# Vision-transformer layer with experts: softmax reciprocals in another PSUM bank, load order at the handover, and weighted groups on GpSimd

## The chip, the cores and the metric

The kernel runs on one core of a Trainium2 chip. The metric is the device time of one execution in microseconds (us), median of several runs. The core has TensorE (matmuls), VectorE, ScalarE, GpSimd and SyncE, each with its own in-order instruction queue; they meet only through semaphores. SBUF is the on-chip memory, PSUM the banks into which TensorE writes, and 16 DMA engines move data to and from device memory.

## The reference

Sixteen images x[16, 4, 128, 256] in float32 go through three parts.

```
tok:  w = x.sum(groups).mean(256); h = gelu(w @ w1.T + b1); w = softmax over 4 groups of (h @ w2.T + b2)
      h[b] = sum over g of x[b, g] * w[g, b]                         # 128 tokens x 256
attn: n = layernorm(h); 16 heads of 16; softmax(q k^T / 4 + relative bias) v;  h += ctx @ Wo.T
moe:  n = layernorm(h); gates = softmax(n @ Wg + bg), the best 2 of 8 experts, normalised
      h += sum over the 2 experts of gate * (gelu(n @ W1[e] + b1[e]) @ W2[e] + b2[e])
```

## The kernel before

The 128 tokens of an image lie on the 128 partitions. The work has three stages.

**Setup** loads the first images and turns the weights.

**Image steps.** step(i) for i = 0 to 16 is a software pipeline over three images, written out by hand on each engine: the front of image i (project_qk, project_v, key masks, scores, biased scores, exponentials of chunks 0 and 1), the back of image i-1 (exponentials of chunks 2 and 3, transposes called context, values, reciprocals, normalise), and the late part of image i-2 (out_project, residual, second norm, gate logits). The four groups of an image are weighted and added one or two images ahead: ScalarE writes the first weighted group (first_group(i + 2), line 553) and VectorE adds groups 1 to 3 in select_groups(i + 1) (line 1107), followed by the statistics of the first norm. GpSimd computes the two rstd (line 434), half of the masked keys (mask_keys, line 267), and in steps 7 to 15 sends out the token records of batches already ranked, by indirect DMA (scatter_records, line 445). The table record_steps says which: two DMAs a step, but four in steps 12 and 14. Ahead of each even-numbered one GpSimd waits until all earlier ones have landed (`scat`).

The softmax reciprocals are widened by VectorE (srcw), turned by TensorE (spread_sums, line 778) into the lower half of the bank psQK, and copied by ScalarE (r_evac, line 567) to rT; VectorE's normalise multiplies psCX by rT. turn_x (line 769) turns the next image's normed tokens into the upper half of psQK, and so waits for r_sb. Then follow values(b, 1), scores(i, 1) and gate_logits in TensorE's queue.

After step 2 TensorE computes the selection logits of images 4 to 15 (select_logits, line 741), once keep_logits(0) has freed the bank (lg_sb); VectorE's select_weights and ScalarE's select_exps make the weights tsel from them, and ScalarE's first_group(4) stands ahead of its step 3.

**Expert tiles.** 39 tiles of 128 token records each: SyncE loads a tile's records (`sel<-meta_dram`) and the expert's first weights (load_w1, 1 MB); GpSimd gathers the tokens (line 482) and scatters the results (line 491); TensorE turns them (turn_xs, line 935) and multiplies (hidden, line 947, and second, line 959). The first 14 tiles need only the records of images 0 to 10. SyncE's queue at the handover is, in order: load_w1(0, 0), load_w1(1, 1), store_xn2(13), one store, the wait for the records' DMAs, records 0 and 1, the wait for s_min and the load of b2 (1 MB), records 2, store_xn2(14), records 3, load_w1(2, 0).

Of the kernel before, what the change touches and what calls it, by code (L numbers as in the profile page):

```python
# [63 lines left out]
def vit_layer_kernel(nc, x, tok_w1, tok_b1, tok_w2, tok_b2, Wq, Wk, Wv, Wo, rel_emb,  # L64
# [8 lines left out]
    with ExitStack() as ctx:  # L73
# [6 lines left out]
        def sem(name):  # L80
            return ctx.enter_context(nc.semaphore(name))
# [119 lines left out]
        waited = {e: sem(f"waited_{n}") for e, n in ((nc.vector.engine, "dve"), (nc.gpsimd.engine, "pool"),  # L201
                                                    (nc.scalar.engine, "act"))}
        dv_const = sem("dv_const")
        setup_ps = sem("setup_ps")
        wT_sb, tokw_sb, b1T_sb = sem("wT_sb"), sem("tokw_sb"), sem("b1T_sb")
        rel_ps = sem("rel_ps")
# [88 lines left out]
        def _(sp):  # L295
# [43 lines left out]
            with sp.Fori(0, E - 2) as e:  # L339
# [5 lines left out]
            load_w2(E - 1)  # L345
            sp.wait_ge(tables_ok, 1)
            load_w1(0, 0)
            load_w1(1, 1)
            store_xn2(B - 3)
            sp.dma_start(sum_dram.ap()[N_TOK:N_TOK + P, :], hcol(0)).then_inc(h_out, 16)  # L350
            sp.wait_ge(scat, 16 * TOPK * EARLY_B)
            load_records(0)
            next_records(1)
            sp.wait_ge(s_min, NCH * B)
            sp.dma_start(relb[:, 0:E * D], b2.rearrange("e d -> (e d)").partition_broadcast(P)) \
                .then_inc(b2_in, 16)
            next_records(2)
            store_xn2(B - 2)
            next_records(3)
            load_w1(2, 0)  # L360
            store_xn2(B - 1)
            next_records(4)
# [26 lines left out]
        def _(pool):  # L389
# [41 lines left out]
            def rstd_of(i, ln, n, done):  # L431
                pool.wait_ge(ln, n)
                pool.wait_ge(dv_const, 1)
                pool.tensor_tensor(rstd[i][:, :], ve[i][:, :], minus_half[:, :], ALU.pow) \  # L434
                    .then_inc(done, 1)

            def scatter_records(g, a, b):
# [4 lines left out]
                for i in range(BATCHES[g][0] * TOPK + a, BATCHES[g][0] * TOPK + b):  # L442
                    if i >= 2 and i % 2 == 0:
# [6 lines left out]
            record_steps = ((7, 0, 0, 2), (8, 0, 2, 4), (9, 0, 4, 6), (10, 0, 6, 8), (11, 1, 0, 2), (12, 1, 2, 6),  # L450
                            (13, 1, 6, 8), (14, 2, 0, 4), (15, 2, 4, 6))

            def step(i, nxt=True, late=True):

                if nxt:
                    rstd_of(0, ln1, LN1_N * (i + 1) + 3, ln1_pow)
                mask_keys(pool, i, 1)
                if late:
                    rstd_of(1, ln2, LN2_N * (i - 2) + 3, ln2_pow)
                for at, g, a, b in record_steps:  # L460
                    if at == i:
                        scatter_records(g, a, b)
# [53 lines left out]
        def _(act):  # L516
# [46 lines left out]
            def r_evac(b):  # L563
                act.wait_ge(r_ps, b + 1)
                if later(b):
                    act.wait_ge(ctx_ok, b)
                act.copy(rT[:, :], psQK[:, 0:DC * S]).then_inc(r_sb, 1)

            def qk_evac(b):
                act.wait_ge(qk_ps, b + 1)  # L570
# [133 lines left out]
        def _(pe):  # L704
# [55 lines left out]

            def turn_x(b):

                if later(b, 1):
                    pe.wait_ge(r_sb, b - 1)
                pe.wait_ge(ln1, LN1_N * (b + 1))
                if later(b):
                    pe.wait_ge(qk_sb, b)
                for c in range(DC):
                    i = pe.transpose(psQK[:, (DC + c) * S:(DC + c + 1) * S], xn1[:, c * P:(c + 1) * P],
                                     ident[:, :])  # L770
                i.then_inc(x1T_ps, 1)

            def spread_sums(b):

                pe.wait_ge(s_wide, b + 1)
                pe.wait_ge(qk_sb, min(b + 2, B) if isinstance(b, int) else b + 2)
                for c in range(DC):
                    i = pe.transpose(psQK[:, c * S:(c + 1) * S],
                                     srcw[:, c * P:(c + 1) * P], ident[:, :])
                i.then_inc(r_ps, 1)  # L780

# [43 lines left out]
            def values(b, w):  # L825
                if w == 0:
                    pe.wait_ge(v_sb, b + 1)
                    if later(b):
                        pe.wait_ge(ctx_ok, b)
                pe.wait_ge(pT_sb, NCH * b + 2 * w + 2)  # L830
                for j in range(2):
                    for n in range(CH):
                        k = 2 * n + j
                        i = pe.matmul(psCX[n * PART:(n + 1) * PART, w * S:(w + 1) * S],  # L834
                                      v_s[:, v_at(w * HPC + k):v_at(w * HPC + k) + PART],
                                      pT[k // CH][:, k % CH * S:(k % CH + 1) * S], start=(j == 0), stop=(j == 1))
                i.then_inc(pv_ps, 2)
# [41 lines left out]
                pe.matmul(psG[:, RKC:RKC + n * E], before[:, :], counts[:, E:(n + 1) * E],  # L879
                          start=False, stop=True).then_inc(rank_ps, 1)  # L880

            def step(i, u, front=True, back=True, late=True, nxt=True, batch=None, sums=False):

                if front:
                    project_qk(i)
# [24 lines left out]
                    values(i - 1, 1)  # L910
                if front:
                    scores(i, 1)
                if late:
                    gate_logits(i - 2)

# [3 lines left out]
            pe.wait_ge(b1T_sb, 1)  # L919
            step(1, 1, late=False, sums=True)  # L920
            image_sums(3, 2)
            step(2, 0)
            pe.wait_ge(lg_sb, 1)
            select_logits(1, NG, B)
            placed = {first + n + 3: g for g, (first, n) in enumerate(BATCHES[:-1])}
            for i in range(3, B - 1):
                step(i, i % 2, batch=placed.get(i))
# [45 lines left out]
                    turn_xs(j + 1, 1 - u, k + u)  # L973
                second(j - 1, 1 - u, e)

            pe.wait_ge(r_sb, B)
            turn_xs(0, 0, 0)
            hidden(0, 0, 0)
            turn_xs(1, 1, 0)
# [23 lines left out]
        def _(dve):  # L1003
# [92 lines left out]

            def select_groups(b, done=None):

                dve.wait_ge(tok_first, b + 1)
                for g in range(1, G):  # L1100
                    if g == 2 and done is not None:
                        top_two(*done)
                    if g == 3 and done is not None:
                        top_index(*done)
                    if g > 1:
                        dve.wait_ge(tok_acc, (G - 1) * b + g - 1)
                    dve.scalar_tensor_tensor(out=hcol(b), in0=xw2[:, bass.ds(b * (G * D) + g * D, D)],
# [311 lines left out]
```

## Time and profile before

| | |
|---|---|
| median of 3 runs | 538.91 us (538.74 to 540.49) |
| profiled execution, own time | 538.68 us |
| its span | 536.9 us |
| TensorE matmul busy | 484.0 us, 90% |
| VectorE busy | 219.0 us, 41% |
| ScalarE busy | 262.6 us, 49% |
| GpSimd busy | 178.9 us, 33% |
| mean granted clock of TensorE | 0.969 |

Times in rows are microseconds from the span's start. PE is TensorE (PEld its weight loads, which overlap its matmuls), DVE VectorE, ACT ScalarE, POOL GpSimd, SPq the DMA queue of SyncE. In a timeline a row is: start, duration, engine, line, operation, out<-in, shape, count, and in brackets the engine's idle time just before it with what ended it. The chain of waits is the work that ended last, followed back from the end.

### The profile page before, as it was taken

Reading aid. Unit: us, or ns where it says so; the run is one execution under the profiler, and the core shown is the slowest. Engines: PE = TensorE matmul, PEld = TensorE weight load, DVE = VectorE, ACT = ScalarE, POOL = GpSimd, SP = SyncE. Lnnn points to the kernel's source line nnn. Section 1 sums busy time; section 2 is a strip of 40 time slices with the busy share of each in tenths; the row PEclk is TensorE's granted clock in tenths of the full one; section 3 lists DMA queues with packets and bytes.
Section 4 is the critical chain, followed back from the end, with each engine's and each line's share of the span. In section 5 each row is a group of like instructions: output and inputs, shape, how many; then the busy total and the mean of one; then the engine's idle time right before and its main releaser. Section 6 shows DMA issues by size and latency. Waiting matters only on the chain.

```text
span 536.9 us, 13085 instructions
## 1 busy us (share of the span) xinstructions
PE 484.0 (90%) x3742; PEld 409.8 (76%) x3743; DVE 219.0 (41%) x1068; ACT 262.6 (49%) x1003; POOL 178.9 (33%) x186
## 2 busy tenths in 40 slices
PE   4779899999999999499999999999999999999980
PEld 2557676666766665289998989999999999999960
DVE  2665788887887887422241111111111111111110
ACT  1347689889998888632432223332233332323310
POOL 3020113233334633213265533333333333333321
PEclk9979899999999999879999999999999999999995
DMA  8890030313313046536656665666766666666515
GB/s 273 244 351 31 21 99 22 102 38 102 85 36 100 22 120 204 172 112 193 183 140 171 194 169 148 187 187 192 195 180 175 165 178 184 195 189 174 138 20 166
DMA packets 51004, 78.61 MB, mean 146 GB/s; under 512 B 10528, under 2 KB 39472, under 8 KB 50768
## 3 DMA queue, kind: packets, MB, share of 16 engines
q1 hardware_dynamic: 40160, 66.80, 38.4%
q0 software_dynamic: 8592, 10.58, 11.8%
q10 hardware_dynamic: 2208, 0.71, 0.6%
q8 instruction: 20, 0.33, 0.3%
q14 instruction: 24, 0.20, 0.2%
HBM read 68.27 MB, written 11.90 MB: 149 GB/s over the span
## 4 chain that ended last, share of the span: by engine, by line
PE 73%; issue 9%; DMA 5%; DVE 4%; POOL 3%; ACT 3%; POOLq 0%; DVEq 0%; SPq 0%; ACTq 0%
PE psVO L959 23%; PE psS L947 12%; PE psP L947 12%; PE psP L822 5%; PE psQK L789 5%; PE psS L812 4%; DMA fold<-xn_dram,sel 3%; PE psCX L834 2%; PE psVO L845 2%; PE psVO L800 2%; PE psQK L935 2%; ACT prob L592 2%; DVE prob L1127 2%; POOL meta_dram L445 2%; PE psG L725 1%
## 5 line engine op out<-in xcount | busy, mean ns | idle before, releaser
L959 PE MATMUL psVO<-xw,prob 128*128 x624 | 141.8, 380 | 0.8 <-DVE fold L1349 0.8
L959 PEld LDWEIGHTS psVO<-xw,prob 128*128 128x128 f32 x624 | 115.5, 190 | 15.8 <-issue 1.2
L491 POOL DMA_INDIRECT sum_dram<-fold,sel x39 | 62.0, 1591 | 163.4 <-DMA sel<-meta_dram 103.6
L592 ACT ACTIVATE prob<-prob,smin 128x128 f32<-128x128 f32 x256 | 100.4, 405 | 6.1 <-DVE smin L1127 5.8
L679 ACT ACTIVATE prob<-psS,b1T 128x128 f32<-128x128 f32 x160 | 45.8, 369 | 99.5 <-PE psS L947 99.5
L679 ACT ACTIVATE prob<-psP,b1T 128x128 f32<-128x128 f32 x152 | 43.5, 369 | 92.6 <-PE psP L947 87.9
L947 PEld LDWEIGHTS psS<-fold,w1c 128*128 128x128 f32 x640 | 76.6, 197 | 1.9 <-DVE fold L1344 1.0
L947 PE MATMUL psS<-fold,w1c 128*128 128x128 f32 x640 | 77.1, 280 | 0.6 <-DVE fold L1344 0.6
L947 PEld LDWEIGHTS psP<-fold,w1c 128*128 128x128 f32 x608 | 70.8, 192 | 0.9
L947 PE MATMUL psP<-fold,w1c 128*128 128x128 f32 x608 | 71.0, 275 | 0.0
L434 POOL TENSOR_TENSOR rstd<-ve,minus_half 128x1 f32<-128x1 f32 x32 | 23.9, 747 | 136.5 <-DVE ve L1090 133.1
L1349 DVE TENSOR_TENSOR fold<-psVO,relb 128x256 f32<-128x256 f32 x39 | 16.6, 425 | 122.1 <-PE psVO L959 118.9
L1344 DVE COPY fold<-psQK 128x256 f32<-128x256 f32 x39 | 16.6, 425 | 112.5 <-PE psQK L935 112.5
L1127 DVE CUSTOM_DVE_ANT_0 prob<-psS,relb 128x128 f32<-128x128 f32 x256 | 56.7, 286 | 13.2 <-PE psS L812 12.5
L592 ACT ACTIVATION_READ_ACCUMULATOR prob<-prob,smin 128x1 f32 x256 | 52.0, 203 | 0.0
L581 ACT COPY pT<-psP 128x512 f32<-128x512 f32 x64 | 36.1, 594 | 20.9 <-PE psP L822 20.9
L482 POOL DMA_INDIRECT fold<-xn_dram,sel x39 | 39.0, 1001 | 19.4 <-issue 10.9
L812 PE MATMUL psS<-kbd,qkT 64*128 64x512 f32 x128 | 37.1, 655 | 4.7 <-DVE smin L1127 2.3
L445 POOL DMA_INDIRECT meta_dram<-meta,pos x32 | 32.4, 1011 | 24.6 <-DMA meta_dram<-meta,pos 12.2
L822 PEld LDWEIGHTS psP<-ident,prob 128*128 128x128 f32 x256 | 28.1, 141 | 15.7 <-issue 8.3
L822 PE MATMUL psP<-ident,prob 128*128 128x128 f32 x256 | 37.9, 280 | 0.7 <-ACT prob L592 0.7
L789 PE MATMUL psQK<-x1T,wT 128*128 128x128 f32 x256 | 34.2, 289 | 0.5 <-ACT x1T L561 0.5
(166 smaller groups left out, 491.7 us busy)
## 6 DMA issues: line engine op xcount, KB each, us to landing
w1c<-in_L_ffn_W SPq DMA_DIRECT2D x39, 1024.0 KB
xw<-in_x SPq DMA_DIRECT2D x16, 512.0 KB, 8.1
xw<-in_L_ffn_W SPq DMA_DIRECT2D x8, 1024.0 KB, 5.9
sum_dram<-h_all SPq DMA_DIRECT2D x17, 128.0 KB
xn_dram<-xn SPq DMA_DIRECT2D x16, 128.0 KB
out<-sum_dram SPq DMA_DIRECT2D x4, 512.0 KB, 5.9
relb<-in_L_ffn_b SPq DMA_DIRECT2D x1, 1024.0 KB, 5.5
sel<-meta_dram SPq DMA_DIRECT2D x39, 2.0 KB
```

What stands on the lines that cost most here:

```text
L445: pool.indirect_dma_start(out=meta_dram.ap()[:, :], out_offset=bass.IndirectOffsetOnAxis(ap=pos[:, i:i + 1], axis=0), in_=meta[:, i * META ...
L482: pool.indirect_dma_start(out=xs[j % 2], out_offset=None, in_=xn_dram.ap()[0:EARLY_B * S if j < EARLY else N_TOK, :], in_offset=bass.Indir ...
L491: pool.indirect_dma_start(out=sum_dram.ap()[0:EARLY_B * S if j < EARLY else N_TOK + P, :], out_offset=bass.IndirectOffsetOnAxis(ap=row_no[ ...
L581: act.copy(pT[c % 2][:, :], psP[c % 2][:, :]).then_inc(pT_sb, 1)
L592: i = act.activation(blk, blk, ACT.Exp, bias=smin[:, k:k + 1], scale=-1.0, accum_out=ssum[:, k:k + 1])
L679: i = act.activation(hT[u][:, c * P:(c + 1) * P], hidden_ps[u][c // 4][:, c % 4 * P:(c % 4 + 1) * P], ACT.Gelu, bias=b1T[:, bass.ds(e * HC ...
L789: i = pe.matmul(psQK[:, (t * DC + oc) * S:(t * DC + oc + 1) * S], wT[t][:, ic * D + oc * P:ic * D + oc * P + P], x1T[:, ic * S:(ic + 1) * ...
L812: pe.matmul(psS[r][:, :], qkT[rows, w * S:(w + 1) * S], kbd[rows, w * CH * S:(w + 1) * CH * S], start=True, stop=True).then_inc(s_ps, 1)
L822: i = pe.transpose(psP[c % 2][:, n * S:(n + 1) * S], pr[:, h * S:(h + 1) * S], ident[:, :])
L947: i = pe.matmul(hidden_ps[u][c // 4][:, c % 4 * P:(c % 4 + 1) * P], w1c[u][:, d * H + c * P:d * H + (c + 1) * P], xsT[:, d * P:(d + 1) * P ...
L959: i = pe.matmul(psVO[:, 0:D], hT[u][:, c * P:(c + 1) * P], xw2[:, bass.ds(e * (HC * D) + c * D, D)], start=(c == 0), stop=(c == HC - 1))
L1127: i = dve.tensor_tensor_reduce(prob[u % 2][:, h * S:(h + 1) * S], psS[c % 2][:, n * S:(n + 1) * S], relb[:, h * S:(h + 1) * S], 1.0, HIGHE ...
```

## The change

Three edits, and a fourth that moves a small piece.

1. spread_sums writes the upper half of the bank psCX instead of the lower half of psQK. r_evac reads there. turn_x no longer waits for r_sb; values(b, 1) does. The waits of spread_sums for qk_sb and of the first tile for r_sb go.
2. SyncE: load_w1(1, 1) and store_xn2(14) move behind records 1 and 2, and the load of b2 behind records 3.
3. For images 5 to 15 GpSimd weights groups 1 to 3 in place with one product over 768 columns and adds them to the first group with three sums, in step b - 2, behind its rstd and ahead of that step's records. VectorE's select_groups(b) keeps only the wait, the statistics and the two operations on the gate logits of a finished image.
4. select_logits for images 4 to 15 moves into step 2, ahead of gate_logits(0), waiting for x2T_sb instead of lg_sb.

```diff
@@ SyncE @@
             load_w1(0, 0)
-            load_w1(1, 1)
             store_xn2(B - 3)
...
             next_records(1)
+            next_records(2)
+            load_w1(1, 1)
+            store_xn2(B - 2)
+            next_records(3)
             sp.wait_ge(s_min, NCH * B)
             sp.dma_start(relb[:, 0:E * D], b2.rearrange("e d -> (e d)").partition_broadcast(P)) \
                 .then_inc(b2_in, 16)
-            next_records(2)
-            store_xn2(B - 2)
-            next_records(3)
@@ GpSimd @@
+            def select_groups(b):
+
+                pool.wait_ge(tok_first, b + 1)
+                pool.wait_ge(tok_acc, (G - 1) * b)
+                x_of = xw2[:, b * (G * D) + D:(b + 1) * (G * D)]
+                x_of = [x_of] + [x_of[:, g * D:(g + 1) * D] for g in range(G - 1)]
+                pool.tensor_tensor(chunks(x_of[0], G - 1, D), chunks(x_of[0], G - 1, D),
+                                   over(tsel[:, B:G * B].rearrange("p (g b) -> p g b", g=G - 1)[:, :, b], D),
+                                   ALU.mult).then_inc(tok_part, 1)
+                pool.wait_ge(tok_part, 2 * (b - NG) - 1)
+                pool.tensor_tensor(x_of[1], x_of[1], x_of[2], ALU.add).then_inc(tok_part, 1)
+                pool.tensor_tensor(hcol(b), hcol(b), x_of[3], ALU.add).then_inc(tok_acc, 1)
+                pool.wait_ge(tok_part, 2 * (b - NG))
+                pool.wait_ge(tok_acc, (G - 1) * b + 1)
+                pool.tensor_tensor(hcol(b), hcol(b), x_of[1], ALU.add).then_inc(tok_acc, 2)
+
             def step(i, nxt=True, late=True):
...
                 if late:
                     rstd_of(1, ln2, LN2_N * (i - 2) + 3, ln2_pow)
+                if NG < i + 2 < B:
+                    select_groups(i + 2)
                 for at, g, a, b in record_steps:
@@ ScalarE @@
-                act.copy(rT[:, :], psQK[:, 0:DC * S]).then_inc(r_sb, 1)
+                act.copy(rT[:, :], psCX[:, DC * S:2 * DC * S]).then_inc(r_sb, 1)
@@ TensorE @@
             def turn_x(b):
 
-                if later(b, 1):
-                    pe.wait_ge(r_sb, b - 1)
...
             def spread_sums(b):
...
-                pe.wait_ge(qk_sb, min(b + 2, B) if isinstance(b, int) else b + 2)
                 for c in range(DC):
-                    i = pe.transpose(psQK[:, c * S:(c + 1) * S],
+                    i = pe.transpose(psCX[:, (DC + c) * S:(DC + c + 1) * S],
@@ values @@
+                else:
+                    pe.wait_ge(r_sb, b + 1)
                 pe.wait_ge(pT_sb, NCH * b + 2 * w + 2)
@@ TensorE's step @@
+                if select:
+                    pe.wait_ge(x2T_sb, i - 1)
+                    select_logits(1, NG, B)
                 if late:
                     gate_logits(i - 2)
...
-            step(2, 0)
-            pe.wait_ge(lg_sb, 1)
-            select_logits(1, NG, B)
+            step(2, 0, select=True)
...
-            pe.wait_ge(r_sb, B)
             turn_xs(0, 0, 0)
@@ VectorE @@
             def select_groups(b, done=None):
 
+                if done is not None:
+                    top_two(*done)
+                if b > NG:
+                    dve.wait_ge(tok_acc, (G - 1) * (b + 1))
+                    norm_stats(0, hcol(b), ln1, LN1_N * b)
+                    if done is not None:
+                        top_index(*done)
+                    return
+                if done is not None:
+                    top_index(*done)
                 dve.wait_ge(tok_first, b + 1)
                 for g in range(1, G):
-                    if g == 2 and done is not None:
-                        top_two(*done)
-                    if g == 3 and done is not None:
-                        top_index(*done)
```

## Rows read from the trace of the kernel before

**Rows 1.** Chain of waits, 133 to 146 us: start, duration, what.
```profile
133.84 1.89 PE psQK L789 x16
...
141.78 0.26 ACT rT L567
...
144.10 0.26 ACT x2T L609
```

**Rows 2.** Timeline of a regular step, 137 to 149 us, all engines.
```profile
137.65 0.69 DVE L267 TENSOR_TENSOR kbd<-qkT,pmask 128x512 f32<-128x512 f32 x1
137.80 0.97 POOL L434 TENSOR_TENSOR rstd<-ve,minus_half 128x1 f32<-128x1 f32 x1 [5.85 <-DVE ve L1090]
...
138.44 0.42 DVE L1156 TENSOR_TENSOR h_all<-h_all,psVO 128x256 f32<-128x256 f32 x1
...
138.75 1.03 POOL L267 TENSOR_TENSOR kbd<-qkT,pmask 128x512 f32<-128x512 f32 x1
...
142.04 0.52 ACT L553 ACTIVATE h_all<-xw,tsel 128x256 f32<-128x256 f32 x1
...
142.21 0.44 PE L769 MATMUL psQK<-ident,xn 128*128 128x128 f32 x2 [0.51 <-ACT rT L567]
...
148.98 1.09 POOL L434 TENSOR_TENSOR rstd<-ve,minus_half 128x1 f32<-128x1 f32 x1 [5.86 <-DVE ve L1090]
```

**Rows 3.** Instructions of lines 1107 and 267: count, ns min/median/max, first and last start.
```profile
L1107 DVE SCALAR_TENSOR_TENSOR h_all<-xw,tsel,h_all x48: 464/478/486, 18.9 to 193.7; 128x256 f32<-128x256 f32 x48
...
L267 POOL TENSOR_TENSOR kbd<-qkT,pmask x16: 1030/1034/1547, 28.7 to 209.1; 128x512 f32<-128x512 f32 x16
```

**Rows 4.** Timeline of GpSimd, ScalarE and VectorE in steps 12 and 13.
```profile
176.90 0.52 ACT L553 ACTIVATE h_all<-xw,tsel 128x256 f32<-128x256 f32 x1
...
177.16 0.98 POOL L445 DMA_INDIRECT meta_dram<-meta,pos  x1 [0.30 <-issue]
...
181.16 0.96 POOL L445 DMA_INDIRECT meta_dram<-meta,pos  x1 [3.01 <-DMA meta_dram<-meta,pos]
...
186.06 0.55 POOL L434 TENSOR_TENSOR rstd<-ve,minus_half 128x1 f32<-128x1 f32 x1
...
187.57 0.29 DVE L1127 CUSTOM_DVE_ANT_0 prob<-psS,relb 128x128 f32<-128x128 f32 x1
...
188.65 0.40 ACT L592 ACTIVATE prob<-prob,smin 128x128 f32<-128x128 f32 x1
```

**Rows 5.** Timeline from step 2 to step 3, 62 to 70 us.
```profile
62.80 0.97 PEld L741 LDWEIGHTS psG<-sel 128*128 128x128 f32 x8 [1.69 <-DVE lg_all L1168]
...
63.68 3.42 PEld L789 LDWEIGHTS psQK<-x1T,wT 128*128 128x128 f32 x16
...
63.90 0.21 DVE L1068 TENSOR_TENSOR sel<-psG,tb 128x48 f32<-128x48 f32 x1 [1.15 <-PE psG L741]
...
68.12 1.06 ACT L581 COPY pT<-psP 128x512 f32<-128x512 f32 x2
...
69.90 0.38 PEld L834 LDWEIGHTS psCX<-pT,v_s 128*32 128x32 f32 x16 [0.33 <-issue]
```

**Rows 6.** Stretch 64 to 66 us: busy per engine, clock, DMA share, GB/s.
```profile
64.00:66.00 2.00, 2.00 (x11) 2.00 (x11) 1.21 (x6) 0.55 (x2) 0.00 (x0) 0.50 0.00 0
```

**Rows 7.** Chain of waits at the handover, 200 to 260 us.
```profile
215.52 3.57 DMA meta_dram<-meta,pos
...
222.37 5.95 DMA fold<-xn_dram,sel
...
229.84 6.03 PE psS L947 x32
```

**Rows 8.** Timeline of SyncE's DMA queue at the handover.
```profile
208.43 1.70 SPq L330 DMA_DIRECT2D w1c<-in_L_ffn_W  x2
...
222.45 0.43 SPq L355 DMA_DIRECT2D relb<-in_L_ffn_b  x1
```

**Rows 9.** Timeline of TensorE at the first tile.
```profile
228.57 0.66 PE L935 MATMUL psQK<-ident,fold 128*128 128x128 f32 x2 [5.90 <-DMA fold<-xn_dram,sel]
```

More of the change, by code:

```diff
@@ L203, in vit_layer_kernel @@
         dv_const = sem("dv_const")
+        tok_part = sem("tok_part")
         setup_ps = sem("setup_ps")
@@ L880, in ranks, with step @@
                           start=False, stop=True).then_inc(rank_ps, 1)
-            def step(i, u, front=True, back=True, late=True, nxt=True, batch=None, sums=False):
+            def step(i, u, front=True, back=True, late=True, nxt=True, batch=None, sums=False, select=False):
                 if front:
```

## The prediction

> **What bounds the kernel now.** I read the busy table first: TensorE works nine tenths of the span, GpSimd a third, VectorE two fifths. Then the chain of waits, which splits the span in two stages. The sixteen image steps end near 222 us, the 39 expert tiles fill the rest, and in the tiles TensorE hardly stops. The change touches no tile instruction, so the question is what happens to the image steps and to the handover.
>
> A regular image step takes 11.18 us (GpSimd's rstd at 137.80 and 148.98 [rows 2]). Its chain goes in a ring: project_qk, transposes and projections, values, scores, then ScalarE's copies of the transposed probabilities and of the reciprocals, its first weighted group, four exponentials, the copy of x2T, and the gate logits ahead of the next project_qk [rows 1]. ScalarE hands over to TensorE at 144.10 + 0.26 = 144.36. Neither VectorE's three weighted adds nor the wait of turn_x on the reciprocals' copy, 0.51 us long [rows 2], has a place in that ring.
>
> **Reciprocals in the context's bank.** turn_x no longer waits for r_sb, but values(b, 1) now does, since it writes the bank that ScalarE's copy reads. So TensorE still waits for the same event (the copy that starts at 141.78 [rows 1]), with turn_x's 0.44 us [rows 2] moved ahead of it. values(1) and scores(1) come up to 0.4 us earlier, but gate_logits, next in TensorE's queue, waits for x2T, which ScalarE copies only after the four exponentials. The gain is swallowed there. I cost it at 0; bounds 0 and -0.4 us a step (12 such steps, -4.8).
>
> **Weighted groups on GpSimd.** VectorE loses three operations of 478 ns per image [rows 3], 11 images: 15.8 us of VectorE time, all ahead of the kbd product, which waits for ScalarE's copy of q and k anyway. Worth 0 in regular steps, perhaps 0.1 in each of the three gate steps (VectorE ends last there), -0.3 together.
>
> GpSimd gains per image one product over 768 columns and three sums over 256. The nearest row is its own kbd product, 512 columns in 1034 ns [rows 3], 2.02 ns a column: 1.55 us for the product, 0.52 us for each sum. Three waits on its own results lie between; rows 4 show 0.30 us between two of its DMA instructions, so I take about 0.25 each: 1.55 + 1.56 + 0.75 = 3.9 us. The bounds are 3.1 (no gaps) and 4.6 (0.55 us a sum, 0.45 a gap).
>
> It starts only when ScalarE's first group of image i+2 is there, 142.04 + 0.52 = 142.56 [rows 2], and ends about 146.5. VectorE's statistics follow; before, they released GpSimd's rstd at 148.98, 2.5 us later, and GpSimd had idled 5.86 us for it [rows 2], so nothing is lost. In steps 7 to 11 and 13 two record DMAs stand behind the select in its queue: 0.2 + 1.0 + 0.30 + 0.98 = 2.5 us (the last two from rows 4, the first two taken as like), to 149.0. That is a tie with 148.98: no cost, but no slack either.
>
> The Trainium skill (GPSIMD Engine Reference, 3.1 Elementwise) speaks against such a move: it gives a two-input add on GpSimd as 1.96 times VectorE's time and keeps elementwise work on VectorE. The trace has 1.03 against 0.69 us for the same product (138.75 and 137.65 [rows 2]), a ratio of 1.5. By the page's ratio the select would be, as an estimate, 6.4 us, and all steps with records would be late by some 2 us; the trace's own ratio decides here.
>
> **Step 12: where it hurts.** This step issues four record DMAs, and the third waits until the first two have landed. Before, the second went out at 177.16, the third after 3.01 us of waiting at 181.16 [rows 4]. Now the select stands in front, and itself waits for the first group that ends at 176.90 + 0.52 = 177.42 [rows 4]. Working: select to 181.3; two DMAs 2.5, to 183.8; landing 3.0, to 186.8; two DMAs 0.96 + 0.30 + 1.0, to 189.1; 0.35 to the rstd of image 14 (0.55, to 190.0); the second half of kbd 1.03, to 191.1; the rstd of image 11, to 191.7. That last one ended at 186.06 + 0.55 = 186.6 before [rows 4]: 5.1 us later. VectorE's queue holds first_norm, second_norm, the masks and then biased(0) behind it, which began at 187.57, and ScalarE's exponentials behind that at 188.65, straight after its own work [rows 4]. So there is no slack: step 13 starts its ring 5.0 us late. Bounds 4.2 (select 3.1) and 5.8.
>
> TensorE idles those 4 to 5 us (turn_xn2 waits for second_norm). After an idle of 1.69 us [rows 5] its granted clock was 0.50, the 1.2 GHz level, in 64 to 66 us [rows 6], and project_qk's weight loads took 3.42 us [rows 5] against 1.89 for the matmuls of a step at full clock [rows 1]. I add 1.5 us for this; bounds 0 and 2.5. Together +6.5.
>
> Steps 14 and 15 get no select, and select(15) in step 13 starts behind the late rstd (191.7) and ends with its two DMAs near 198, while step 14 wants its rstd more than 3 us after that by now, so the delay doesn't grow.
>
> **select_logits(1) earlier.** Before, TensorE waited 1.69 us for lg_sb, then ran select_logits (62.80), then project_qk (63.68) at half clock; values(0) of that step began at 69.90 [rows 5]. Now select_logits runs right behind scores(1), at 62.80 less the idle and the gate logits' half microsecond, near 60.6. VectorE had idled 1.15 us for it when it began the weights at 63.90 [rows 5]; that idle goes, and ScalarE, which waits for the weights, starts 1.1 us earlier. TensorE was the later of the two at values(0); with project_qk at 62.1 it no longer is: ScalarE's second copy ended at 69.18 [rows 5], now at 68.1, and values(0) follows it, -1.75. I take -1.6; bounds -1.1 and -1.8.
>
> **Handover to the tiles.** The records' chain was: DMA of the last early record pair 215.52 + 3.57, records 0, gather 0 issued 222.37 and landed 5.95 us later, hidden(0) 6.03 us [rows 7]; TensorE began at 228.57 after 5.90 us idle [rows 9]. The 1 MB load of b2 was issued at 222.45 [rows 8], beside the gather. Now records 1 and 2 stand in front of w1(1,1) and b2, so the first megabyte is issued near 224.1. No row shows a gather without load beside it; the nearest from below is the record pair, 3.57 us from the start of its second issue, from above the 5.95 itself. I take 3.6, nearer the pair, because the first 1.7 us after the issue are free of load: -2.4. The record pair before it flew beside both w1 loads (208.43 [rows 8]); now only one is there, worth 0 to 1 us, I take 0.4. Sum -2.8, bounds -1.0 and -4.0. TensorE then still idles 3.1 us, so hidden(0) keeps its 6.03 us. w1(1,1) is needed only behind hidden(0), 7 us later: hidden.
>
> **Sum.** 0 - 0.3 + 6.5 - 1.6 - 2.8 = +1.8 us on the profiled execution's 538.68: 540.5. The median of the runs stands 0.23 higher, so 540.7.
>
> **Rivals.**
> (a) *The handover pays more than the stall costs* (faster). Place: from 207 to 234 us. If the gather and the last records save 4.0 us or more, TensorE idles below 1.9 us, close to the 1.69 us of rows 5, and hidden(0) may run in 3.6 instead of 6.03: -6.4 instead of -2.8. It decides from about 4 us saved. For it: the load of b2 leaves the gather's way, and the gather is most of the idle. Against: w1(0,0) still flies beside the records. With the stall at 6.5: -1.9, 537.0; without the clock's loss in step 13: 535.5.
> (b) *GpSimd's port.* VectorE's kbd product (two SBUF inputs, 137.65) and GpSimd's rstd (137.80) overlapped, and the rstd took 0.97 us [rows 2] instead of 0.55 [rows 4]; but the residual add out of PSUM (138.44, 0.42) overlapped with GpSimd's kbd (138.75, 1.03), which took no longer than its median [rows 2, 3]. The select runs beside biased, which reads PSUM and SBUF. If these excluded each other, each regular step would lose about 1 us: +11, 551. The Trainium skill (SBUF — State Buffer, SBUF: two separate sides) calls the shared pair an exclusive lock, but only against VectorE operations with two SBUF inputs or in a two-port mode; by that rule biased is free, and the rows agree as far as they go.
> (c) *The released wait pays after all:* 0.38 us in 12 steps, -4.6, and with the rest 536.1. Against it stands the chain, where turn_x is absent.
> (d) *The stall isn't there,* because the records of step 12 find GpSimd free: only if the select took well under 1 us. Then 538.9 - 4.7 = 534.2.
>
> **How the numbers follow.** Forecast 0.57 (its own range 538.5 to 543.5), (a) 0.18, (b) 0.10, (c) 0.08, (d) 0.03, small mixtures the rest. Range 535.8 to 545.0: it takes in (a), (c) and the bounds of the stall and the clock, and leaves (b) and (d) out. Measurement tells about 0.3% (1.6 us) from no change. Faster by more: (a) mostly, (c), (d): 0.23. Within: the lower half of the forecast: 0.31. Slower: 0.46.
>
> **What would show it.** In the changed kernel: GpSimd's select lasting near 3.9 us and starting when ScalarE's first group ends; a GpSimd queue in step 12 whose fourth record DMA ends near 188 and an rstd behind it, with ScalarE idle for 4 to 5 us ahead of step 13's exponentials on VectorE's smin; regular steps of 11.2 us still; project_qk of step 3 1.5 us earlier; gather 0 in under 4 us. It is wrong if step 13 starts without idle, if the regular steps change by more than 0.2 us, or if TensorE idles as long as before at the handover.

## The result and the profile after

The changed kernel takes 542.5 us (median of 8 runs, 540.76 to 543.14) against 539.46 us before (8 runs, 538.74 to 540.74): a ratio of 1.0043 with a 95% interval of 1.0027 to 1.006, that is 1.5 to 3.2 us slower. The prediction was 540.7 us, range 535.8 to 545.0, with "slower" the likeliest of the three signs. Its sum was made against the profiled execution: 538.68 and +1.8. The profiled execution of the changed kernel took 540.76 us, so +2.1 there. This execution was also the fastest of its eight; the rows below account for the +2.1, and what the other runs have on top is shown by no profile.

The step times come from the weight loads of project_qk, which open every step on TensorE. The table gives the length of each stretch in us.

| stretch (from project_qk to project_qk) | before | after | difference | forecast |
|---|---|---|---|---|
| step 1 | 13.18 | 12.85 | -0.3 | 0 |
| step 2, to 63.68 and to 61.59 | 13.51 | 11.70 | -1.8 | -1.6 |
| step 3 | 12.69 | 12.54 | -0.15 | 0 |
| gate steps 6 and 10 together | 22.81 | 23.23 | +0.4 | -0.2 |
| regular steps | 11.18 | 11.17 | 0 | 0 |
| step 13, to the project_qk of step 14 | 11.35 | 17.97 | +6.6 | +6.5 for both |
| step 14 | 11.89 | 13.47 | +1.6 | |
| handover, project_qk of step 15 to the first tile's transposes | 25.59 | 21.75 | -3.8 | -2.8 |
| tiles, to the end of the span | 308.4 | 307.8 | -0.6 | 0 |

The differences add up to +1.9 us, as much as the spans (536.9 and 538.8) differ. The two large terms are those of the forecast, each larger than forecast, in opposite directions. (In a gate step the expert gates of a batch of finished images are computed as well; the handover is the passage from the last image step to the first expert tile.)

The GpSimd queue through steps 12 and 13, where [rows 4] had shown two record DMAs, a wait of 3.01 us and two more:

```profile
175.65 1.47 POOL L460 TENSOR_TENSOR xw<-xw,tsel 128x768 f32<-128x768 f32 x1 [2.05 <-ACT h_all L572]
...
178.78 0.73 POOL L468 TENSOR_TENSOR h_all<-h_all,xw 128x256 f32<-128x256 f32 x1 [0.17 <-POOL h_all L465]
179.68 1.04 POOL L446 DMA_INDIRECT meta_dram<-meta,pos  x1 [0.17 <-issue]
181.02 0.98 POOL L446 DMA_INDIRECT meta_dram<-meta,pos  x1 [0.30 <-issue]
183.42 0.96 POOL L446 DMA_INDIRECT meta_dram<-meta,pos  x1 [1.41 <-DMA meta_dram<-meta,pos]
...
185.66 0.57 POOL L435 TENSOR_TENSOR rstd<-ve,minus_half 128x1 f32<-128x1 f32 x1
186.21 1.03 POOL L268 TENSOR_TENSOR kbd<-qkT,pmask 128x512 f32<-128x512 f32 x1
187.21 0.55 POOL L435 TENSOR_TENSOR rstd<-ve,minus_half 128x1 f32<-128x1 f32 x1
187.73 1.46 POOL L460 TENSOR_TENSOR xw<-xw,tsel 128x768 f32<-128x768 f32 x1
189.27 0.72 POOL L464 TENSOR_TENSOR xw<-xw 128x256 f32<-128x256 f32 x1
189.95 0.78 POOL L465 TENSOR_TENSOR h_all<-h_all,xw 128x256 f32<-128x256 f32 x1
190.90 0.72 POOL L468 TENSOR_TENSOR h_all<-h_all,xw 128x256 f32<-128x256 f32 x1 [0.17 <-POOL h_all L465]
```

The select of image 14 lasts from 175.65 to 179.51, 3.86 us, and every record DMA of the step comes after it. The third one waits only 1.41 us, less than half of before. The rstd of image 11 (187.21) ends at 187.76, and the select of image 15 starts at once behind it. What this does to VectorE is in VectorE's timeline of the same stretch:

```profile
186.35 3.80 DVE L1112 TENSOR_SCALAR xn<-h_all,mv,rstd 128x256 f32<-128x256 f32 x2 [1.71 <-POOL rstd L435]
190.07 0.73 DVE L1220 TENSOR_TENSOR hot<-e_no,picked 128x48 f32<-128x48 f32 x1
...
191.09 0.29 DVE L1151 CUSTOM_DVE_ANT_0 prob<-psS,relb 128x128 f32<-128x128 f32 x1
```

The two normalisations (`xn`, the first norm of image 14 and the second norm of image 11) take 3.80 us together. In the regular step at 138.37 the same pair takes 0.75 us. The group of line 1112 over the whole execution says how unusual that is (count, ns min/median/max); the 3.00 us are the first of the two, from 186.35 to 189.35, and the second lasts 0.88 us from 189.27:

```profile
L1112 DVE TENSOR_SCALAR xn<-h_all,mv,rstd x32: 405/409/3000, 23.0 to 241.8; 128x256 f32<-128x256 f32 x32
```

ScalarE waits for the biased scores; its timeline:

```profile
192.16 0.40 ACT L611 ACTIVATE prob<-prob,smin 128x128 f32<-128x128 f32 x1 [5.42 <-DVE smin L1151]
```

and TensorE for the second normalisation; its weight loads:

```profile
190.20 0.29 PEld L878 LDWEIGHTS psG<-ident,xn 128*128 128x128 f32 x2 [4.78 <-DVE xn L1112]
...
195.82 3.53 PEld L805 LDWEIGHTS psQK<-x1T,wT 128*128 128x128 f32 x16
```

The stretches of 2 us show TensorE idle from 186 to 190 and its granted clock behind that (window, length, busy of PE, PEld, DVE, ACT, POOL, clock, DMA share, GB/s):

```profile
186.00:188.00 2.00, 0.00 (x0) 0.00 (x0) 1.65 (x1) 0.74 (x3) 2.00 (x4) 1.00 0.02 1
188.00:190.00 2.00, 0.00 (x0) 0.00 (x0) 2.00 (x2) 0.00 (x0) 1.92 (x3) 0.83 0.00 0
190.00:192.00 2.00, 1.80 (x20) 1.31 (x20) 1.89 (x12) 0.00 (x0) 1.66 (x3) 0.50 0.34 114
...
196.00:198.00 2.00, 2.00 (x11) 2.00 (x11) 1.82 (x15) 1.78 (x9) 0.00 (x0) 0.50 0.14 29
198.00:200.00 2.00, 2.00 (x13) 2.00 (x13) 0.35 (x4) 0.31 (x1) 0.56 (x1) 0.61 0.00 0
200.00:202.00 2.00, 2.00 (x13) 1.82 (x12) 0.69 (x1) 2.00 (x8) 1.55 (x1) 1.00 0.04 8
```

The clock is at the 1.2 GHz level from 190 to past 198, so the end of step 13 and the opening of step 14 run at half clock: project_qk's loads take 3.53 us instead of 1.87.

The handover, in the chain of waits of the changed kernel, answers to [rows 7]; the third row is of TensorE's timeline and answers to [rows 9]:

```profile
222.53 2.12 DMA meta_dram<-meta,pos
...
227.85 2.97 DMA fold<-xn_dram,sel
...
232.35 6.08 PE psS L966 x32
```

```profile
231.07 0.66 PE L954 MATMUL psQK<-ident,fold 128*128 128x128 f32 x2 [2.09 <-DMA fold<-xn_dram,sel]
```

The gather lands in 2.97 us instead of 5.95 and the last record pair in 2.12 instead of 3.57. TensorE idles 2.1 us instead of 5.9, and hidden(0) still takes 6.1 us.

Last, the step 2 to step 3 passage, in TensorE's weight loads, against [rows 5]:

```profile
60.26 0.97 PEld L760 LDWEIGHTS psG<-sel 128*128 128x128 f32 x8 [0.81 <-ACT x2T L628]
...
61.59 1.87 PEld L805 LDWEIGHTS psQK<-x1T,wT 128*128 128x128 f32 x16
```

### The profile page after: what moved, and what is told of

Read it like the earlier page. It is cut to its first block, busy times and chain, and to the rows that moved or that the text cites. A ratio compares the mean times of both kernels' runs of the same rounds, so it can differ in the third digit from the quotient of the medians.

```text
span 538.8 us, 13118 instructions
## 1 busy us (share of the span) xinstructions
PE 485.4 (90%) x3742; PEld 411.6 (76%) x3743; DVE 212.9 (40%) x1035; ACT 262.4 (49%) x1003; POOL 216.4 (40%) x230
## 3 DMA queue, kind: packets, MB, share of 16 engines
q0 software_dynamic: 8592, 10.58, 11.7%
## 4 chain that ended last, share of the span: by engine, by line
PE 68%; issue 10%; DVE 7%; POOL 4%; ACT 4%; DMA 4%; POOLq 0%; DVEq 0%; SPq 0%; ACTq 0%
PE psVO L978 23%; PE psS L966 12%; PE psP L966 12%; PE psQK L805 4%; PE psP L838 4%; PE psS L828 3%; DVE prob L1151 2%; DMA fold<-xn_dram,sel 2%; ACT prob L611 2%; POOL meta_dram L446 2%; PE psVO L816 2%; PE psVO L863 2%; PE psQK L954 2%; PE psG L884 1%; DVE xn L1112 1%
## 5 line engine op out<-in xcount | busy, mean ns | idle before, releaser
L611 ACT ACTIVATE prob<-prob,smin 128x128 f32<-128x128 f32 x256 | 100.0, 401 | 11.7 <-DVE smin L1151 11.7
L435 POOL TENSOR_TENSOR rstd<-ve,minus_half 128x1 f32<-128x1 f32 x32 | 19.5, 608 | 82.0 <-DVE ve L1108 80.2
L611 ACT ACTIVATION_READ_ACCUMULATOR prob<-prob,smin 128x1 f32 x256 | 50.8, 198 | 0.0
```

The costliest lines, as they stand in the source:

```text
L611: i = act.activation(blk, blk, ACT.Exp, bias=smin[:, k:k + 1], scale=-1.0, accum_out=ssum[:, k:k + 1])
```

## The experiments

The theory behind the runs: the change is three gains or nothings (loads, select_logits, bank) and one loss, the select that stands ahead of step 12's four record DMAs. The rival was that GpSimd's work costs everywhere, through the port that it shares with VectorE. The kernel before was timed again beside the experiments: 538.98 us (7 runs) beside the first four, 539.44 us (26 runs) beside the others; each ratio is against the one beside it.

**The select of image 14 between the record pairs.** GpSimd sends the first pair, then adds the groups while the pair is in flight, then sends the second pair.

```diff
+                if i == 12:
+                    scatter_records(1, 2, 4)
+                    select_groups(14)
+                    scatter_records(1, 4, 6)
+                    return
                 if NG < i + 2 < B:
                     select_groups(i + 2)
```

> The changed kernel with one edit: in step 12 GpSimd sends the first pair of records ahead of image 14's weighted groups and the second pair behind them, instead of all four behind. If the queue of step 12 is the cause of the late step 13 (my theory), the pair falls into GpSimd's 2.1 us of waiting for the first group, its landing is hidden under the select, and the next rstd comes about 182.7 instead of 185.7 us: step 13 takes 11.3 to 12.0 us instead of 18.0, step 14 no longer runs project_qk at half clock, and the time is 534 to 535.5 us against 542.5 of the changed kernel. If the stall came from the weighted groups running beside VectorE's norms (the shared port), the order of the records does little: 540 to 542.5.

Measured 530.85 us (4 runs, 530.03 to 532.94) against 538.98: ratio 0.9845 (0.9815 to 0.9875). All GpSimd selects are still there, in every regular step; only the order in one step differs from the changed kernel. GpSimd's timeline:

```profile
173.94 1.04 POOL L446 DMA_INDIRECT meta_dram<-meta,pos  x1 [0.23 <-issue]
175.28 0.98 POOL L446 DMA_INDIRECT meta_dram<-meta,pos  x1 [0.30 <-issue]
176.27 1.49 POOL L460 TENSOR_TENSOR xw<-xw,tsel 128x768 f32<-128x768 f32 x1
...
180.31 0.99 POOL L446 DMA_INDIRECT meta_dram<-meta,pos  x1 [0.15 <-issue]
...
184.33 0.55 POOL L435 TENSOR_TENSOR rstd<-ve,minus_half 128x1 f32<-128x1 f32 x1 [0.16 <-DVE ve L1113]
```

The wait for the landing is gone (the select fills it), the rstd of image 11 now waits for VectorE and not VectorE for it, and project_qk goes 177.97, 189.30, 200.99: step 13 takes 11.33 us and step 14 takes 11.69. The stall is the loss: the rival, for which selects cost in every step, is out. (Inside the stalled step GpSimd does hold VectorE up; the experiment on the select of image 15 below gives its share.) The run is 3 to 5 us better than expected: the expectation had counted on 7 to 8.5 us against the changed kernel, and the medians are 11.7 apart. The profiled executions are 7.8 us apart (540.76 and 532.94); steps 13 and 14 alone give 8.4 of it (23.02 us for 31.44), and the rest goes the other way. The first profile is of the fastest run of its kernel and the second of the slowest of its own, so where the rest of the medians' difference lies is shown by neither.

**The groups back on VectorE**, the rest of the change kept.

```diff
-                if NG < i + 2 < B:
-                    select_groups(i + 2)
```

(and VectorE's select_groups as before.)

> The changed kernel with the weighted groups 1 to 3 back on VectorE; the other three edits stay. My theory: image steps as before the change but 2.2 us earlier from step 3 on, no stall in step 13, handover 3.8 us shorter, so 539.5 - 6.0 = 533.5 us. If the handover's saving in the changed kernel was only the other side of the stall (records and loads had more time to land), it goes too: about 537.

Measured 531.5 us (530.45 to 534.42), ratio 0.9869 (0.9822 to 0.9915). That is 2 us better than expected. The intervals of this run and the first overlap for the most part. So moving the adds to GpSimd gains nothing that can be measured even where it does no harm: the "0" of the forecast for regular steps holds from this side too. It also says that the three other edits are worth about 7.5 us together, and that the handover's saving doesn't need the stall.

**The groups on GpSimd alone**, on the kernel before.

```diff
+                if NG < i + 2 < B:
+                    select_groups(i + 2)
                 for at, g, a, b in record_steps:
```

> The kernel before with only the weighted groups on GpSimd. My theory: the whole cost stands here, 8.2 us in steps 13 and 14 and 0.4 in the gate steps, and nothing is given back: 548 us. If part of the stall is absorbed at the handover (where DMAs and not the image steps end last), 543 to 545.

Measured 548.32 us (545.57 to 550.86), ratio 1.019 (1.0148 to 1.0232). Step 13 takes 17.95 us (180.56 to 198.51), the same as in the changed kernel, and step 14 takes 13.32. The profiled execution was the fastest of the four (545.57), so of the median's +9.3 us its rows account for 6.9. The row of project_qk at the start of step 14:

```profile
198.51 3.30 PEld L808 LDWEIGHTS psQK<-x1T,wT 128*128 128x128 f32 x16
```

The loss belongs to this edit alone and needs none of the others.

**The load order alone**, on the kernel before.

```diff
-            load_w1(1, 1)
             store_xn2(B - 3)
...
             next_records(1)
+            next_records(2)
+            load_w1(1, 1)
```

(with b2 behind records 3, as in the change.)

> The kernel before with only the new order of SyncE's loads and records. My theory: gather 0 lands in 3 us instead of 6, and the last record pairs a little earlier: 539.5 - 3.8 = 535.7 us, with TensorE idle 2 us instead of 6 ahead of the first tile. If the saving needs the stall, 538 or more; if TensorE's clock then holds at 2.4 GHz through the first tile, 533.5.

Measured 534.54 us (534.1 to 535.66), ratio 0.9916 (0.9887 to 0.9944): -4.4 us, where I had the handover at -2.8. Its chain of waits:

```profile
217.11 2.12 DMA meta_dram<-meta,pos
219.96 1.62 DMA sel<-meta_dram
222.47 2.80 DMA fold<-xn_dram,sel
...
226.81 5.88 PE psS L947 x32
```

The gather lands in 2.80 us here and in 2.85 to 2.97 in the other four kernels with the new order whose chains show it, against 5.80 to 6.04 in the four with the old order. The record pair lands in 2.10 to 2.12 us in all five with the new order. With the old one it took 2.98, 3.25, 3.57 and, in the kernel with the groups on GpSimd alone, 6.21 us. So both gains belong to the load order, the gather's is the steadier, and the pair's depends on which execution with the old order it is set against.

**select_logits alone**, on the kernel before.

```diff
-            step(2, 0)
-            pe.wait_ge(lg_sb, 1)
-            select_logits(1, NG, B)
+            step(2, 0, select=True)
```

> The kernel before with only select_logits for images 4 to 15 moved ahead of gate_logits(0). My theory: TensorE's 1.7 us of idle and the half clock behind it go, step 2 takes 11.7 instead of 13.5 us from project_qk to project_qk: -1.9 us, 537.2. If later waits take it back, 538.5 to 539.5.

Measured 536.09 us (7 runs, 535.0 to 539.12), ratio 0.9936 (0.9916 to 0.9957), -3.4 us. The profile shows project_qk of step 3 at 62.78 and a start of step 2 at 51.03, 11.75 us apart, against 13.51 before: -1.8 us, the forecast's mechanism. The other 1.6 us of the median have no row: this profiled execution was the slowest of the seven, and longer in the tiles.

**The bank alone**, on the kernel before.

```diff
-                act.copy(rT[:, :], psQK[:, 0:DC * S]).then_inc(r_sb, 1)
+                act.copy(rT[:, :], psCX[:, DC * S:2 * DC * S]).then_inc(r_sb, 1)
```

(and the waits of TensorE as in the change.)

> The kernel before with only the reciprocals in the context's bank, and the wait for r_sb moved from turn_x to values(b, 1). My theory: the step's ring does not pass through turn_x, so nothing: 539.2 within 0.7 us. If the released wait pays 0.38 us in 12 steps, 534.6.

Measured 538.45 us (12 runs, 537.4 to 540.1), ratio 0.9982 (0.996 to 1.0005): -1.0 us, with no change at all inside the interval. TensorE's weight loads in the regular step at 140 us show why there is no more:

```profile
140.99 0.25 PEld L767 LDWEIGHTS psQK<-ident,xn 128*128 128x128 f32 x2
141.77 0.38 PEld L833 LDWEIGHTS psCX<-pT,v_s 128*32 128x32 f32 x16 [0.53 <-ACT rT L567]
142.49 0.33 PEld L809 LDWEIGHTS psS<-kbd,qkT 64*128 64x128 f32 x4 [0.35 <-issue]
143.96 0.52 PEld L865 LDWEIGHTS psG<-wg_s,x2T 128*128 128x128 f32 x4 [1.14 <-ACT x2T L609]
```

turn_x runs ahead of the wait, the wait for the reciprocals' copy stands in front of values instead, and what values and scores gain is lost again at gate_logits, which waits 1.14 us for ScalarE's x2T. Rival (c) is out. What is there lies in single steps: 12.85 instead of 13.18 us for step 1, 11.68 instead of 11.89 for step 14.

**The first record pair ahead of the select in every step**, on the changed kernel.

```diff
+                for g, a, b in mine:
+                    scatter_records(g, a, min(b, a + 2))
                 if NG < i + 2 < B:
                     select_groups(i + 2)
+                for g, a, b in mine:
+                    if b > a + 2:
+                        scatter_records(g, a + 2, b)
```

> The changed kernel with the first pair of each step's records ahead of the weighted groups, in every step and not in step 12 alone. My theory: the pair falls into GpSimd's 2.1 us of waiting for the first group; only step 12 was short, so the time is that of the version with step 12 alone, 530.9, within 1 us. If the tie of steps 7 to 11 (records end just when the rstd is due) costs something each time, 529 to 530.

Measured 532.44 us (530.84 to 534.27), ratio 0.987 (0.9835 to 0.9904). The median is 1.5 us above the expected 530.9, half a microsecond outside the margin given, but its interval and the first run's overlap. So in the steps with two record DMAs no effect of the order can be told from none, as the forecast's "tie" had it.

**The select of image 15 held back until the masks of step 13 are done**, on the changed kernel. This is the test of the 3.80 us pair: the stall by the queue stays, and VectorE's delay by the select goes.

```diff
+                if i == 13:
+                    pool.wait_ge(gate_step, GATE_N * 2 + MASKS_AT)
                 if NG < i + 2 < B:
                     select_groups(i + 2)
```

> The changed kernel with one wait more: in step 13 GpSimd starts the weighted groups of image 15 only when VectorE has finished second_norm and the masks of that step. The records of step 12 stay where they are. In the changed kernel's trace VectorE's two normed outputs of that step last 3.80 us instead of 0.75, and end only when GpSimd's product over 768 columns and its first sum are through. If GpSimd's weighted groups hold VectorE up there (shared port), biased(0) of step 13 starts 2.4 us earlier and the step takes 15.6 us instead of 18.0; time 540.1 instead of 542.5. If VectorE waited for something else (GpSimd's rstd alone), nothing changes or the added wait costs: 542.5 to 544.

Measured 538.51 us (10 runs, 537.98 to 541.2), ratio 0.9993 (0.9972 to 1.0014), 4.0 us below the changed kernel by the medians (542.5 and 538.51, measured at different times) where 2.4 were expected. The profiled executions are 2.3 us apart, and only 1.1 of that lies in steps 13 and 14. VectorE's timeline:

```profile
185.96 1.05 DVE L1114 TENSOR_SCALAR xn<-h_all,mv,rstd 128x256 f32<-128x256 f32 x1 [1.70 <-POOL rstd L435]
187.55 0.41 DVE L1114 TENSOR_SCALAR xn<-h_all,mv,rstd 128x256 f32<-128x256 f32 x1 [0.55 <-POOL rstd L435]
187.88 0.20 DVE L1222 TENSOR_TENSOR hot<-e_no,picked 128x48 f32<-128x48 f32 x1
```

With GpSimd quiet, the second normalisation takes 0.41 us again and `hot` 0.20. From the end of the rstd (187.41) to the first biased operation (188.37) it is 0.96 us; in the changed kernel, from 187.76 to 191.09, it is 3.33. So the GpSimd select held VectorE up by 2.4 us. Step 13 took 15.65 us (expected 15.6). Half of this is given back in step 14, which took 14.65 us instead of 13.47: TensorE resumes earlier but runs at half clock just as far. Windows of this run:

```profile
190.00:192.00 2.00, 1.70 (x4) 0.54 (x4) 1.62 (x6) 2.00 (x11) 1.83 (x3) 0.50 0.68 146
...
196.00:198.00 2.00, 2.00 (x11) 2.00 (x11) 0.40 (x1) 0.76 (x2) 0.53 (x2) 0.50 0.04 8
198.00:200.00 2.00, 2.00 (x10) 1.75 (x9) 0.29 (x1) 1.73 (x7) 1.19 (x1) 0.68 0.00 0
```

The clock comes back between 198 and 200 us here as in the changed kernel, although TensorE is back at work at 188.0 and not at 190.2. So more of step 14 lies before that point: the transposes and part of the out_project as well as project_qk.

**The clock at the handover.** The first experiment's profile bears on rival (a), which put the return of the clock in hidden(0) below 1.9 us of idle time. Its row of TensorE's timeline and its windows:

```profile
222.89 0.41 PE L959 MATMUL psQK<-ident,fold 128*128 128x128 f32 x2 [1.66 <-DMA fold<-xn_dram,sel]
223.92 5.47 PE L971 MATMUL psS<-fold,w1c 128*128 128x128 f32 x32 [0.61 <-DVE fold L1373]
```

```profile
222.00:224.00 2.00, 0.49 (x3) 0.28 (x3) 0.68 (x4) 0.00 (x0) 0.34 (x1) 1.00 0.59 81
224.00:226.00 2.00, 2.00 (x12) 2.00 (x13) 0.21 (x2) 0.00 (x0) 0.96 (x1) 0.66 0.93 342
226.00:228.00 2.00, 2.00 (x12) 2.00 (x11) 0.00 (x0) 0.77 (x4) 0.00 (x0) 0.50 1.11 408
228.00:230.00 2.00, 2.00 (x17) 1.95 (x17) 0.36 (x1) 0.85 (x4) 0.00 (x0) 0.99 0.98 405
```

Idle pauses of 1.66 and 0.61 us, with TensorE busy 0.49 of 2 us at 222 to 224, and the clock still falls, if later. hidden(0) took 5.47 us here, 6.08 in the changed kernel, against 3.57 for the same work at full clock in later tiles. In the kernel with the groups back on VectorE TensorE was idle for only 0.18 us ahead of the first tile's transposes and 1.19 us behind them, and the clock fell there too:

```profile
222.00:224.00 2.00, 0.72 (x3) 0.51 (x4) 1.77 (x10) 0.48 (x2) 0.70 (x1) 0.76 0.59 141
```

Its hidden(0) took 6.78 us. No run here kept the clock through the handover.

## Why the prediction came out as it did

**The regular steps, the bank, rival (b) and (c).** Right. Regular steps stay at 11.17 us; the select takes 3.86 us (forecast 3.9) from the end of ScalarE's first group. That agreement is partly luck: the product took 1.47 us (forecast 1.55), the three sums 2.19 (1.56), and the gaps 0.2 (0.75). The 6.4 us that the prediction sets beside its 3.9 comes without its working; scaled as its own sum is, with 1.96 for 1.5 and the same gaps, it is 4.8. Where the step has a record pair, the first rstd stands right behind it (146.01 + 0.98, then 147.01) and the step is no longer than before: the tie was one. Rival (b) asked whether VectorE's biased operations and GpSimd's select exclude each other. They don't: at 191.09 biased runs beside the select at its usual 0.29 us.

**Steps 13 and 14: the mechanism right, all three of its terms wrong in size.** Counted from the project_qk of step 13:

| term | forecast | measured |
|---|---|---|
| rstd of image 11 later | +5.1 | +3.0 (ends 9.91 us in, was 6.9) |
| VectorE between that rstd and biased | 0 (-0.1) | +2.4 |
| half clock | +1.5 | +2.8 (1.26 in step 13, 1.58 in step 14) |
| sum | +6.5 | +8.2 |

The first two errors almost cancel: the first biased operation came 5.4 us later, against the 5.1 that the forecast had for the rstd and with it for the start of step 13. That this number came out was luck.

The first term was too high. Measured from project_qk (179.70 before, 177.85 after), the select was forecast to end 1.6 us in and the first pair 4.1 us in; they ended 1.66 and 4.15 us in. Then the forecast carried the landing of the pair over unchanged, 3.0 us, where it took 1.41: 1.6 of the 2.1 us by which the term is too high, the rest being small gaps that weren't there. Why it landed sooner stays open. Before the change the stores of step 12 went out just ahead of the pair's second DMA (176.32 and 176.86 against 177.16), and in the changed kernel they are over by then. But with the stores at the same distance the wait was 3.48 and 3.47 us with the loads and with select_logits alone, and only 1.84 with the bank alone and 1.77 with the groups back on VectorE. So the stores alone don't set it, and the 3.0 carried over was one value of several.

The second term is the step that failed. The forecast said of select(15) that it "starts behind the late rstd (191.7) and ends with its two DMAs near 198, while step 14 wants its rstd more than 3 us after that", and so cost it at nothing. It asked only who waits for the select and not whom the select holds up while it runs. In a regular step the select falls beside VectorE's biased operations and ctxT, which read PSUM and kept their times (0.29 and 0.43 us at 142.28 and 140.91). The stall shifted it against VectorE's queue, so that it fell on the two normalisations and the masks, whose tensor operands are in SBUF. The experiment that held it back showed the 2.4 us. The Trainium skill (SBUF — State Buffer, "SBUF: two separate sides") has this as a rule: VectorE and GpSimd share a port pair, which one instruction locks for its whole length. The trace agrees in that the operation was held: 3.00 us for one of 0.41. The Trainium skill names there operations with two SBUF inputs and those in a two-port mode, and further down ("Who interferes with whom") tensor_scalar among the candidates; the forecast weighed the rule on biased alone, where it is free. One instruction's length isn't enough for the 3.00 us, though. The operation started 0.14 us into GpSimd's kbd product (186.21) and ended 0.16 us behind the product that GpSimd had begun at 187.73, so three GpSimd instructions in a row went ahead of it. In the run that held the select back it started 0.15 us into the same kbd product and took 1.05 us. What lets several go first isn't shown by any run here.

Not every operation on SBUF is held. The statistics of the norm, one SBUF input of the same 128x256, take 427 to 429 ns all 32 times in the kernel before, also where GpSimd's kbd product (184.91 to 185.94) runs beside them:

```profile
185.04 0.43 DVE L1085 BATCH_NORM_STATS2 st<-h_all 128x6 f32<-128x256 f32 x1
```

The third term lay above the upper bound of 2.5. The forecast had taken it from one project_qk at half clock (3.42 for 1.89 us). The half clock lasted over 8 us here and also held the transposes, values and scores of step 13 and the project_qk of step 14. From ScalarE's first exponential to the next project_qk it was 3.66 us instead of 2.40 (188.65 to 191.05 before), the 1.26; step 14 has the 1.58, nearly all of it project_qk's 3.53 for 1.87.

**select_logits.** Forecast -1.6, measured -1.8 in step 2, in the changed kernel and alone (11.70 and 11.75 for 13.51), and -0.15 in the next step. The other -0.3, in step 1, is the bank's: the kernel with the bank alone has it too. TensorE's wait shrank from 1.69 to 0.81 us, and the clock stayed at full (1.00 in every 2 us from 58 to 68): project_qk takes 1.87 us instead of 3.42 [rows 5]. The size and the place were right.

**The handover.** Forecast -2.8, bounds -1.0 to -4.0, measured -3.8. The gather was put at 3.6 us "nearer the pair" and took 2.97; the record pair was given 0.4 us and gained 1.45 (3.57 to 2.12). That second term is the larger error; one of the two megabyte loads beside the pair was gone, and the landing took less by more than a third of the 3.57 (by less in the executions with the old order that took 2.98 and 3.25). Against the 4.4 us that the two gained, the last pair went out 0.7 us later behind project_qk of step 15 (13.24 us for 12.58). Idle time fell to 2.1 us and the clock wasn't saved, so rival (a) came true in its first half (about 4 us saved) and not in its second. With idle times of 1.66 and 1.19 us, below the 1.9 at which rival (a) expected the clock to hold, it fell as well.

**Gate steps.** Forecast -0.1 each, measured +0.26 and +0.16. In step 6 VectorE's small gate operations stand beside the select (gate_sum 0.54 us instead of 0.17), which fits the lock; a wait of 0.41 us ahead of biased in the same step isn't explained and stays open.

**The sum of the parts.** Alone they measured +9.3, -4.4, -3.4 and -1.0 us, together about +0.5, and the whole change measured +3.0. Each has an uncertainty of 1 to 2.3 us, and they were timed at different times, so this gap of 2.5 us isn't an interaction that is shown. The profiles give +2.1.

The right sign, and a size of +2.1 for +1.8 us by the profiled executions (+3.0 by the medians), came with errors that cancelled: +1.7 us in the stall and +0.6 in gate steps 6 and 10, against -1.0 at the handover, -0.7 in steps 1 to 3 and -0.6 in the tiles.

## What to carry to other kernels

Work moved to an idle engine must be laid against that engine's queue step by step: the average step hid the select entirely, and the one step in which the queue already waited for a transfer paid 8 us for it. In that step, put the work between the issue and the wait, where it costs nothing: with five lines this turned a loss of 0.4% into a gain of 1.5% over the kernel before. And a VectorE normalisation (tensor_scalar) or two-input product whose operands are all in SBUF can be held while GpSimd's elementwise work runs beside it, so a shift of the two against each other changes costs that no dependency shows. Statistics, and operations that read PSUM, weren't held here.

## What the hardware showed that I had not expected

- VectorE's normalisation of 128x256 with one SBUF tensor and two per-partition scalars took up to 3.00 us beside three GpSimd instructions in a row (kbd product, rstd, the select's product), 1.05 beside a kbd product alone and 0.41 otherwise; a 128x48 product with two SBUF inputs took 0.73 instead of 0.20. Custom operations that read PSUM and SBUF kept their 0.29 us.
- GpSimd's product over 768 columns with a broadcast factor took 1.47 us (1.9 ns a column), its sums of two full 256-column inputs 0.73 us (2.9 ns a column). My estimate had 2.02 ns for both; the sums' 0.63 us too little was made up by gaps 0.55 us shorter than assumed.
- GpSimd waited 1.41 us for the landing of a pair of indirect record DMAs in step 12 after the change, 3.01 us in the same step before, 1.77 to 3.48 in four other kernels with the pair in the same place, and 4.3 to 4.7 us in step 14 of all ten kernels, where stores and a 1 MB load went out beside it.
- After the stall the clock stayed at the 1.2 GHz level for over 8 us although TensorE had work again, and with TensorE back at work 2.2 us sooner (188.0 instead of 190.2) it came back in the same window of 2 us.
